# A chunked linear-attention layer and a gated feed-forward: the last tile turned by TensorE, its gates in two banks, another order of work in the last ticks

## The reference

```python
def step(W, kv):
    kc, vc = kv
    z = jnp.einsum('bhsd,bhde->bhse', kc, W)
    grad = jnp.einsum('bhsd,bhse->bhde', kc, (z - vc) * inv_n)
    return (W - LR * grad, z)
```

```python
x = _layernorm(x + attn(x))                      # called x1 below
x = _layernorm(x + (silu(x1 @ gate_w.T * gate_s) * (x1 @ up_w.T * up_s)) @ down_w.T * down_s)
```

## Time and profile before

| | us |
|---|---|
| median of 3 executions | 2120.65 (2120.45 to 2123.52) |
| the profiled execution | 2128.82 |
| its span, first to last instruction | 2126.9 |
| TensorE busy | 1910.0, 90% of the span |
| VectorE, ScalarE, GpSimd busy | 1358.6, 924.4, 650.7 |
| mean granted TensorE clock | 0.953 of full |
| from gate 30.2, tick 33's first, to the end of the span | 2030.2 to 2126.9 |

### The profile page before, as it was taken

One profiled execution on the slowest core, in us unless ns is written; L12 is line 12 of the kernel. 1 busy time (PEld: TensorE's weight loads), 2 busy tenths in 40 slices (PEclk: granted clock), 3 DMA queues, 4 the chain that ended last, 5 costly groups with the idle time before them and its releaser, 6 DMA issues.

```text
span 2126.9 us, 53841 instructions
## 1 busy us (share of the span) xinstructions
PE 1910.0 (90%) x21656; PEld 1500.9 (71%) x21656; DVE 1358.6 (64%) x2878; ACT 924.4 (43%) x2258; POOL 650.7 (31%) x778
## 2 busy tenths in 40 slices
PE   5548999999999999999999999999999999998887
PEld 3326777777777777777777777777777777777665
DVE  3465676667666666676676666667666666766542
ACT  2324444444444444444444444444444444444421
POOL 1012323333333333333323323332332333333222
PEclk9679999999999999999999999999999999999998
DMA  8843444554444445444434544443454444444320
GB/s 297 266 124 117 141 120 136 152 157 127 133 138 138 131 144 155 130 143 136 142 118 142 153 149 124 137 144 116 140 153 147 125 144 138 135 122 133 94 66 21
DMA packets 307978, 294.02 MB, mean 138 GB/s; under 512 B 42896, under 2 KB 256144, under 8 KB 307728
## 3 DMA queue, kind: packets, MB, share of 16 engines
q1 hardware_dynamic: 302768, 273.26, 42.7%
q10 hardware_dynamic: 4960, 17.30, 2.2%
HBM read 156.19 MB, written 142.87 MB: 141 GB/s over the span
## 4 chain that ended last, share of the span: by engine, by line
PE 61%; DVE 24%; DMA 5%; issue 5%; SPq 3%; POOL 1%; ACT 1%; DVEq 0%; POOLq 0%; ACTq 0%
PE gu_acc L704 26%; PE work L690 18%; PE down_acc L716 11%; DVE err L881 7%; DVE x_lo L917 4%; PE z_acc L663 3%; PE state_acc L678 3%; DVE hid L888 2%; DVE x_tok L898 2%; SPq L252 2%; DVE turned L821 2%; DVE x_tok L816 1%; DVE stats L802 1%; DMA landed<-zT_scr 1%; DMA zT_scr<-turned 1%
## 5 line engine op out<-in xcount | busy, mean ns | idle before, releaser
L443 POOL TENSOR_TENSOR hid_lo<-hid,hid_hi 128x256 fp32r<-128x256 f32 x352 | 269.2, 765 | 1013.1 <-ACT hid_hi L534 1013.1
L704 PE MATMUL gu_acc<-x_hi,gw 128*128 128x256 f32 x1408 | 400.1, 315 | 104.3 <-DVE x_lo L917 65.8
L881 DVE TENSOR_TENSOR err<-z_acc,v_rows 32x256 f32<-32x256 f32 x1024 | 429.3, 419 | 100.9 <-PE z_acc L663 65.2
L500 ACT ACTIVATE state<-state_acc 32x256 f32<-32x256 f32 x1028 | 383.7, 373 | 111.3 <-PE state_acc L678 91.5
L704 PEld LDWEIGHTS gu_acc<-x_hi,gw 128*128 128x128 f32 x1408 | 275.0, 195 | 170.0 <-DVE hid L888 74.3
L888 DVE SCALAR_TENSOR_TENSOR hid<-gu_acc,up_scale,hid 128x256 f32<-128x256 f32 x352 | 168.9, 480 | 314.8 <-ACT hid L524 311.0
L524 ACT ACTIVATE hid<-gu_acc,gate_scale 128x256 f32<-128x256 f32 x352 | 166.6, 473 | 456.9 <-PE gu_acc L704 454.9
L704 PE MATMUL gu_acc<-x_hi,uw 128*128 128x256 f32 x1408 | 364.4, 289 | 0.0
L704 PE MATMUL gu_acc<-x_lo,uw 128*128 128x256 f32 x1408 | 363.4, 289 | 0.0
L704 PE MATMUL gu_acc<-x_lo,gw 128*128 128x256 f32 x1408 | 362.5, 288 | 0.0
L716 PE MATMUL down_acc<-dw,hid_hi 128*128 128x512 f32 x704 | 282.3, 401 | 0.9 <-POOL hid_lo L443 0.9
(11 more groups left out here) (64 smaller groups left out, 2122.9 us busy)
## 6 DMA issues: line engine op xcount, KB each, us to landing
x_fm<-xT SPq DMA_DIRECT2D x64, 256.0 KB, 3.5
k_scr<-k_tok SPq DMA_DIRECT2D x32, 512.0 KB, 3.4
kT_scr<-turned SPq DMA_DIRECT2D x128, 128.0 KB, 2.9
kT<-kT_scr SPq DMA_DIRECT2D x32, 512.0 KB, 3.5
k_rows<-k_scr SPq DMA_DIRECT2D x512, 32.0 KB, 2.0
v_rows<-v_scr SPq DMA_DIRECT2D x512, 32.0 KB, 2.1
z_scr<-v_rows SPq DMA_DIRECT2D x32, 512.0 KB, 3.1
z_tok<-z_scr SPq DMA_DIRECT2D x512, 32.0 KB, 1.8
```

The lines of the kernel that those rows point to most:

```text
L443: pool.tensor_tensor(hid_lo[m % RING][:], hid[m % 2][:], hid_hi[m % RING][:].bitcast(F32), ALU.subtract).then_inc(hid_lo_ready, 1)
L500: act.activation(state[q, :, e].rearrange("p (r g) e -> p r g e", r=2), state_acc[q, :, 0:P].rearrange("p r (g e) -> p r g e", e=HEAD), AC ...
L704: mm = pe.matmul(gu_acc[:, k * TOK:(k + 1) * TOK], lhsT=w[:, c, m * P:(m + 1) * P].bitcast(dt), rhs=part[:, c].bitcast(dt), start=(c == 0 ...
L881: dve.tensor_tensor(err[q, g:g + 2, :, :].rearrange("p a (r h) e -> p a r (h e)", r=2), z_acc[q, :, 0:P].rearrange("p r (a c) -> p a r c", ...
```

## The change

The kernel's lines move by the inserted ones: L704 becomes L740, L716 becomes L752, L888 becomes L941, L902 becomes L955, L917 becomes L970, L898 becomes L951, L816 becomes L869, L802 becomes L855, L690 becomes L722.

Ticks up to 32 keep their order. For tick 33 (`WITHOUT_SCAN`) and tick 34 (`END`) the tables have entries of their own. A value is (age, piece): the tile is t - age.

```diff
+USUAL, WITHOUT_SCAN, END = None, NT + 1, NT + 2
+GATE_UP = {...
+           WITHOUT_SCAN: {0: (3, 2), 1: (3, 3), 2: (3, 4), 3: (3, 5), 4: (3, 6), 5: (3, 7), 6: (3, 8), 8: (3, 9),
+                          9: (3, 10), 11: (2, 0), 12: (2, 1), 13: (2, 2), 14: (2, 3), 15: (2, 4)},
...
+def unit_at(table, t, s):
+    age, m = table.get(t, table[USUAL]).get(s, (0, -1))
+    return (t - age, m) if m >= 0 and within(t - age) else None
...
+        def gu_bank(n, m):
+            return z_acc[:, 1, :] if m % 2 and (n == LAST or n == LAST - 1 and m >= 3) else gu_acc[:]
+        def turned_zn(n, b):
+            if n == LAST:
+                return state_acc[:, b, :].rearrange("p (c a t) -> p c a t", c=NC, t=HEAD)
+            return by_token(landed, b)
...
-                if within(o):
+                if within(o) and o != LAST:
                     store_znT(o)
...
-                if m >= 1 or n >= 1:
+                if n == LAST - 1 and m == 3:
+                    pe.wait_ge(z_saved, NS * NT)
+                if n == LAST - 1 and m >= 3 or n == LAST and m >= 1:
+                    pe.wait_ge(hid_ready, NM * n + m - 1)
+                elif m >= 1 or n >= 1:
                     pe.wait_ge(hid_ready, NM * n + m)
...
+            def turn_last(src, b, ready, done):
+                pe.wait_ge(ready, 2 * LAST + b + 1)
+                for c in range(NC):
+                    mm = pe.transpose(state_acc[:, b, c * P:(c + 1) * P], src[:, b, c * P:(c + 1) * P], eye[:])
+                mm.then_inc(done, 1)
...
+                    if o == LAST and s == 5:
+                        turn_last_zn()
+                    if o == LAST and s == 10:
+                        turn_last_x1()
...
-                    if within(yd) and s == 13:
+                    if within(yd) and s == (13 if t != WITHOUT_SCAN else 11):
                         scale_y(yd)
-                    if within(o) and s == 13:
+                    if within(o) and s == (13 if o != LAST else 10):
                         low_x1(o, 0)
...
-                    if within(o) and s == 0:
+                    if within(o) and s == (0 if o != LAST else 3):
                         dve.wait_ge(z_tok_in, 256 * (o + 1))
```

More of the change, by code:

```diff
@@ L466, in tick @@
                         inverse_root(1, o)
[L467 to L471, removed]
+                    if unit_at(LOW, t, s):
+                        low_hid(*unit_at(LOW, t, s))
+                    if within(o) and s == (1 if o != LAST else 4):
                         inverse_root(0, o)
@@ L598, in tick @@
                         copy_v(t + 1, 0)
[L599 to L602, removed]
+                    if unit_at(GATE_UP, t, s):
+                        gate(*unit_at(GATE_UP, t, s))
                     if within(sc) and s % 2 == 0 and s != 14:
                         save_z(sc, s // 2)
-                    if within(o) and s == 5:
+                    if within(o) and s == (5 if o != LAST else 6):
                         high_zn(o, 1)
@@ L748, in project_o, with turn_last_zn, turn_last_x1 @@
                 project(b, wo, o_done)
+            def turn_last(src, b, ready, done):
[3 more added lines that the diff above has]
+                mm.then_inc(done, 1)
+            def turn_last_zn():
+                pe.wait_ge(state_ready, 4 * NS * NT + 4)
+                for b in range(BATCH):
+                    turn_last(z_tok, b, zn_ready, zn_turned)
+            def turn_last_x1():
+                pe.wait_ge(zn_low, 2 * NT)
+                for b in range(BATCH):
+                    turn_last(x1_tok[LAST % 2], b, x1_ready, x1_turned)
             def tick(t, ffn_dt=None, first=0, last=SLOTS):
-                sc, o, f1, f2 = t - 1, t - 2, t - 2, t - 3
+                sc, o = t - 1, t - 2
                 for s in range(first, last):
@@ L774, in tick @@
                         project_k(t + 1, 0)
-                    if within(f2) and s in LATE_DOWN:
-                        down(f2, LATE_DOWN[s], ffn_dt)
-                    if within(f1) and s in EARLY_DOWN:
-                        down(f1, EARLY_DOWN[s], ffn_dt)
+                    if unit_at(DOWN, t, s):
+                        down(*unit_at(DOWN, t, s), ffn_dt)
                     if within(t + 1) and s in (13, 14):
@@ L955, in tick @@
                         normalize(1, o, x1_tok[o % 2], x_tok, x1_ready)
+                    if within(o) and o != LAST and s == 9:
                         turn_x1(o, 0)
@@ L980, in tick @@
                         moments_of(0, o)
-                    if within(o) and s == 1:
+                    if within(o) and s == (1 if o != LAST else 4):
                         normalize(0, o, z_tok, z_tok, zn_ready)
```

76 lines of the change are left out of this document (44 added, 32 removed).

## The result

| | before | changed |
|---|---|---|
| median of 15 executions, us | 2121.93 (2119.82 to 2130.96) | 2110.05 (2105.97 to 2119.09) |
| ratio | | 0.9941 (0.9929 to 0.9953) |
| the profiled execution, its span | 2128.82, 2126.9 | 2110.19, 2108.0 |
| gate 30.2 starts | 2030.2 | 2027.4 |
| gate 30.2 to down 31.10, "the stretch" below | 85.3 | 69.2 |

By the ratio the kernel is faster by 12.5 us, with 10.0 to 15.1 as the interval (the medians are 11.9 apart); 15.7 was forecast. Two later comparisons gave 0.9957 (0.9944 to 0.9971) and 0.9954 (0.9940 to 0.9968), 9 and 10 us.

What follows compares the result with a forecast made beforehand. TensorE's chain was taken to bound the kernel, with 23.7 of 86.6 us idle or slow clock. Gains of 8.2 up to gate 31.0 and 7.55 in tile 31 made 15.7: 2120.65 - 15.7 = 2104.9, range 2102 to 2111.

Steps and rivals of the forecast that it cites:

- The layout: From gate 30.2 to down 31.10, the changed order laid out with profiled durations, each instruction starting once engine and inputs are free.
- long turns: Turns of zn and x1 on TensorE at the upper bound of 3.4 us each: 3.4 more, 2108.3.
- a long low part: Low part of x1 before gate 31.0 at 1.4 us for 0.70: gate 31.0 would start 1.3 later.
- rivals A: TensorE's clock falls at a turn; 4.3 us behind x1's turn or 1.8 for a shorter slow stretch, 2109; chance 0.14.
- Rival B: Gates keep their 3.24 us because the hidden tile's low part comes late; 18 gates at 0.42, 2112.5; chance 0.08.
- the last one of the sum: Taking 15.7 from the median, 0.4% below the profiled 2128.82; claimed to change the sum by less than 0.1.
- Two banks: A gate waits for the product of the gate before the last; gate and down take 2.82 us for 3.24.
- The way of x1: Stores issued at 2061.64, low parts ending just before gate 31.0 at 2075.47; the chain leaves TensorE there.
- The turns: zn and x1 turned on TensorE, 8 blocks each, 1.7 us a turn, between 0.95 and 3.4.
- The uncovered addition: Before the second projection of tile 31, TensorE waits for the first one's addition, 0.95 us idle.
- The low part: Low part of x1 before gate 31.0 takes 0.70 us, with the scaling behind it and nothing of GpSimd beside it.
- C: Slower: clock falls at zn's turn and short waits keep it down, adding some 40 us, 2145; chance 0.03.

Runs made afterwards that it cites:

- e1: The kernel before, without an edit, for a second trace: median 2121.84 us, ratio 1.0002, stretch 82.0 us.
- e8: The kernel before, without an edit, for a third trace: 2121.74 us in one execution, stretch 81.9 us.
- e12: The changed kernel, without an edit, a third time: median 2111.55 us, ratio to before 0.9954, stretch 69.1 us.
- e2: The changed kernel, without an edit, a second time: median 2113.93 us, ratio to before 0.9957, stretch 69.2 us.
- e3: The changed kernel with one bank for gates everywhere, turns and order kept: median 2115.87 us, ratio to before 0.9975, stretch 75.0 us.
- e9: The kernel before with only the low part of x1 put ahead of the sum in every tick: median 2062.56 us, ratio 0.9726, stretch 76.0 us.
- e4: The changed kernel with the last tile's z and x1 turned through DMA as before: median 2124.30 us, ratio to before 1.0011, stretch 84.9 us.
- e10: The changed kernel with the edits of e7 and e6, and tile 31's bias addition moved to slot 6: median 2054.82 us, ratio to before 0.9690.
- e6: The changed kernel with gate 30.8 between the two projections: 2108.37 us in one execution, stretch 68.8 us.
- e7: The changed kernel with the low part of x1 ahead of the sum in every tick: median 2058.97 us, ratio to before 0.9702.
- e11: The changed kernel with two GpSimd additions started to run beside the low part of x1: 2109.67 us in one execution, stretch 69.1 us.
- e5: The changed kernel with each turn's transposes issued six times, 48 for 8: 2116.56 us in one execution, stretch 77.0 us.

## Why the prediction was right, and where it was off

From gate 30.2, in us, laid out and measured in the changed kernel:

| event | laid out | measured |
|---|---|---|
| turn of zn starts | 16.0 | 16.1 |
| first projection | 20.5 | 20.6 |
| second projection | 24.3 | 24.5 |
| turn of x1 | 33.7 | 34.0 |
| gate 31.0 | 37.1 | 36.6 |
| down 31.10 | 69.6 | 69.2 |

- *The layout* held to 0.5 us at each of these. Forecast for the stretch was 85.3 less 15.7; it is 85.3 less 16.1.
- *The range* of 2102 to 2111 holds the result, 2110.05, only just, and not for its reasons. Its upper part was kept for long turns, a long low part, and rivals A and B, and none of these came; the forecast's own bounds added up end at 2109.6. The two repeats, 2113.93 and 2111.55, lie above it. That the range held is partly luck.
- *The step that failed is the last one of the sum*, "The median is 0.4% below that execution, which changes this sum by less than 0.1". The profiled execution was 8 us above the median, and 3.3 us of that lay in the very stretch, as a slow clock in two places where e1 and e8 have a full one. The gain was worked out against a cost that the median doesn't contain. From a stretch of 82 it would have been 12.4, inside the first interval and e12's (up to 12.7), just above e2's (up to 11.9).
- *Two banks*: 2.82 a gate, as laid out; 5.7 us (e3). Rival B is out.
- *The way of x1* through DMA was named as a place where the chain leaves TensorE. In the kernel before it was not: e9 leaves it in place, and the whole wait in front of gate 31.0 is gone. The 4.4 us were the sum ahead of the low part and the low part's length. With fewer gates to cover it, in the new order, that way does cost (e4).
- *The turns*: taken at 1.7, they are 1.03, near the lower bound of 0.95; where nothing interrupts one, the next instruction starts 0.79 after it (e10), below that bound. The "two halves" of a block did not come: the trace has 8 instructions for 8 blocks. What was gained there was mostly lost elsewhere: the normalisation took 2.60 beside the bias addition, where 1.0 was laid out and 1.6 allowed for, and down 30.10 waits 0.49 for its low part, which a turn of 1.7 would have covered.
- *The uncovered addition* between the projections: 0.95 laid out, 0.93 measured; covering it gives 0.6 (e6).
- *The low part* at 0.70: right. Two causes were named, and either is enough: the order, with the residual out of its way (e7, both inputs outside PSUM), and the input from PSUM, beside a neighbour (e11).
- *The clock*: 1.00 throughout, three times over. Rival A did not come, not even in the one execution with turns of 48 transposes (e5). C has nothing for it.
- *The parts do not add up.* Taken out of the changed kernel, the turns are worth 15.7 us of the stretch (e4) and the bank 5.7 (e3); put alone into the kernel before, the exchange is worth 6.0 (e9); all together give 12.8. What a part is worth depends on what else is in place: with the ways through DMA the rest of the change would have brought nothing (e4).

Not foreseen: that the exchange of low part and sum alone brings half of what the whole change gives in the stretch (e9), though rows 1, 7 and 8 show what stands in its place, and that in the other ticks it is worth over four times the whole change (means 2111.0 and 2058.3).

## What to carry to other kernels

Look at the profiled execution's distance from the median before subtracting anything from the median; if a term of the sum is a slow clock, take a second trace and compare the granted clock in the stretch. A wait removed at the end of a program is worth its length once; when its cause (here an instruction behind another on its engine, beside a neighbour) stands in every tick, mend it there first. Before a transfer is blamed for a wait, look whether its data had landed and what stood ahead of the instruction that reads them. Scan banks that lie free at the end are good for a second accumulator and for transposes on TensorE, at 0.11 us a block here.

## What the runs showed of the hardware

- A float32 transpose of 128x128 on TensorE lasts 0.27 us by its own record and costs 0.11 back to back (1.03 for 8 and 5.40 for 48, with the last one's latency), and 48 of them left a clock of 1.00 at 1.00.
- The granted clock, once fallen, does not come back at the same moment in each execution of the same program: behind the same wait of 4.4 us its mean was 0.50 in 9.6 us (before), 0.81 and 0.80 in 9.7 us (e1, e8). Nor does it fall each time: in front of the first projection a wait of 1.81 us was followed by 0.61 (before), one of 1.57 by 1.00 (e8).
- VectorE's subtraction of 128x512 with both inputs outside PSUM took 0.68 to 0.69 us without GpSimd's residual beside it (e7), and 1.40 as its median in the order in which the residual runs beside it (changed kernel, e11); with one input in PSUM it took 0.69 beside a GpSimd addition (e11). The normalisation of z took 2.60 us beside the bias addition and 0.99 without (changed kernel, e10).
- Kernels with transposes on TensorE had 0.35 us more outside their span (2.18 for 1.84). Why is open.
